# Four heads per slot in tiles without relative scores, and one program for the shared and the routed experts

## The reference

```python
q, k, v = (proj(W, b) for ...)              # 16 heads of 8
idx = clip(r[None, :] - r[:, None], -128, 128) + 128
scores = (q @ k^T + einsum('bhqd,qkd->bhqk', q, rel_k[idx])) / sqrt(8)
w = softmax(scores)
out = w @ v + einsum('bhqk,qkd->bhqd', w, rel_v[idx])
x = x + layernorm(out @ Wo.T + bo)          # its input is layernorm(x)

logits = h @ w_router.T                     # h = layernorm(x), 16 experts, top 1
expert = (up * silu(gate)) @ down_proj[e]   # on sigmoid(score) * h
shared = silu(h @ w_gate.T) * (h @ w_up.T) @ w_down.T
x = x + layernorm(shared + expert)
```

## Time and profile before

| | |
|---|---|
| median of 3 timed runs | 1821.07 us (1820.16 to 1823.48) |
| the profiled execution | 1817.03 us |
| its span, first to last instruction | 1815.3 us |
| mean granted TensorE clock | 0.964 |
| busy: PE, DVE, ACT, POOL | 1625.7, 1256.4, 1107.1, 532.7 us |
| slot loop, first and last exponential | 135.0 to 1463.9 us |
| second block, first load | 1594.0 us |

### The profile page before, as it was taken

One profiled execution on the slowest core, in us unless ns is written; L12 is line 12 of the kernel. 1 busy time (PEld: TensorE's weight loads), 2 busy tenths in 40 slices (PEclk: granted clock), 3 DMA queues, 4 the chain that ended last, 5 costly groups with the idle time before them and its releaser, 6 DMA issues. The chain is left out here.

```text
span 1815.3 us, 64460 instructions
## 1 busy us (share of the span) xinstructions
PE 1625.7 (90%) x26621; PEld 1209.2 (67%) x26621; DVE 1256.4 (69%) x3502; ACT 1107.1 (61%) x2059; POOL 532.7 (29%) x1114
## 2 busy tenths in 40 slices
PE   2889999999999999999999999999999988776672
PEld 1337767676777677767776777777677765476662
DVE  5996668787778878777878787877753444246555
ACT  2437767676767676767676766777557632265441
POOL 5422021314142223222321323231101135604435
PEclk9999999999999999999999999999999998889876
DMA  2467855756553555445444654563357342243420
GB/s 61 143 168 201 178 164 109 198 106 166 103 146 69 131 101 145 96 117 128 98 112 104 143 105 120 99 158 53 66 99 209 73 116 69 63 111 95 128 90 26
DMA packets 490854, 211.89 MB, mean 117 GB/s; under 512 B 332391, under 2 KB 464164, under 8 KB 490560
## 3 DMA queue, kind: packets, MB, share of 16 engines
q1 hardware_dynamic: 475968, 165.77, 40.6%
q0 software_dynamic: 14592, 42.00, 6.7%
HBM read 105.73 MB, written 102.85 MB: 115 GB/s over the span
## 5 line engine op out<-in xcount | busy, mean ns | idle before, releaser
L934 ACT ACTIVATE w<-sc,escale 128x512 f32<-128x512 f32 x1024 | 686.1, 686 | 400.6 <-PE sc L731 248.5
L1135 DVE TENSOR_REDUCE mx<-mix 128x1 f32<-128x512 f32 x960 | 646.8, 686 | 242.5 <-PE mix L711 233.1
L710 PE MATMUL mix<-WE 128*128 128x512 f16 x960 | 395.7, 412 | 23.7 <-DVE mx L1135 15.6
L724 PE MATMUL sc<-QC,KC 104*128 104x128 f16 x4096 | 400.6, 221 | 6.2 <-ACT w L934 3.5
L750 PE MATMUL pv<-w,VC 128*9 128x128 f32 x8192 | 380.7, 274 | 2.1 <-issue 2.1
L724 PEld LDWEIGHTS sc<-QC,KC 104*128 104x128 f16 x4096 | 270.6, 98 | 164.1 <-issue 74.3
L711 PE MATMUL mix<-Wn,WE 128*128 128x256 f16 (+1 forms) x960 | 289.4, 301 | 0.0
L750 PEld LDWEIGHTS pv<-w,VC 128*9 128x9 f32 x8192 | 174.5, 90 | 144.6 <-issue 128.9
L925 ACT ACTIVATE WE<-qp,hmask 128x256 f16<-128x256 f16 x512 | 249.0, 500 | 24.7 <-PE sc L711 21.2
L757 PE MATMUL rel<-w,Rv 128*32 128x128 f32 x5120 | 259.4, 273 | 0.5 <-issue 0.5
L731 PE MATMUL sc<-QT,Wt 96*128 96x64 f16 x5120 | 258.5, 192 | 0.0
(11 more groups left out here) (224 smaller groups left out, 1846.6 us busy)
## 6 DMA issues: line engine op xcount, KB each, us to landing
qm_d<-ks POOLq DMA_DIRECT2D x48, 512.0 KB, 4.4
QT<-qm_d SPq DMA_DIRECT2D x32, 768.0 KB
kt_d<-ks SPq DMA_DIRECT2D x48, 256.0 KB
KC<-kt_d SPq DMA_DIRECT2D x128, 96.0 KB
xs_d<-zrow SPq DMA_DIRECT2D x5, 2056.0 KB, 12.3
vs_d<-vst SPq DMA_DIRECT2D x16, 576.0 KB
VC<-vs_d SPq DMA_DIRECT2D x32, 288.0 KB
orl_d<-rel_s SPq DMA_DIRECT2D x512, 8.0 KB
```

The costliest lines, as they stand in the source:

```text
L710: nc.tensor.matmul(nat[:], lq, kn[b2][:, KEYS_AT[t]:KEYS_AT[t] + S], start=True, stop=False, skip_group_check=True)
L724: mm = nc.tensor.matmul(bank[:, P * g:P * g + P], KC[j][:, b2, g, 0 if near else 1, :], qc[:, g, :, 32 * q8:32 * q8 + 32], start=(g == 0), ...
L934: nc.scalar.activation(w[tile % 2][:, slot % 4, slot // 4 % 2].rearrange("p h q -> p (h q)"), sc[slot % 2][:], ACT.Exp, scale=escale[:, 0: ...
L1135: nc.vector.tensor_reduce(mx[:, k:k + 1], nat[:], AX.X, ALU.max).then_inc(s["mx_done"], 1)
```

## The change

1. In far tiles a slot is now one group of four heads against all 128 queries, and `scores` makes one matmul of 512 columns. `exponentials` writes it to the same layout of `w`, so in pieces of 32 queries: `p h u q` is read, `p u h q` is written. `values` is unchanged.
2. `expert_phase` is gone. Its instructions stand at the end of each engine's program in the first block. Its tiles use the banks of the slot loop, and its buffers lie in one tensor, `shared_part`, over those of keys, queries and values. The ring of weights has 7 places. SyncE's order is new, the matmul and the reads of the expert numbers lie between the last units, and the first weight copies ahead of the last unit's `copy_y`.
3. The two roots of the last half pair run on VectorE, and the steps are no longer in GpSimd's order between the units' scatters.
4. The root of a group takes 12 steps instead of 15, and the last group is finished in two halves of four tiles (`ENDINGS`).

```diff
-            for g in range(4):
-                mm = nc.tensor.matmul(bank[:, P * g:P * g + P], KC[j][:, b2, g, 0 if near else 1, :], qc[:, g, :, 32 * q8:32 * q8 + 32],
-                                      start=(g == 0), stop=not near, skip_group_check=True)
+            if not near:
+                mm = nc.tensor.matmul(bank[:], KC[j][:, b2, q8, 1, :], qc[:, q8], start=True, stop=True, skip_group_check=True)
             if near:
+                for g in range(4):
+                    nc.tensor.matmul(bank[:, P * g:P * g + P], KC[j][:, b2, g, 0, :], qc[:, g, :, 32 * q8:32 * q8 + 32],
+                                     start=(g == 0), stop=False, skip_group_check=True)
...
+            if abs(tile // 4 - tile % 4) <= 1:
+                weights, products = w[tile % 2][:, part, b2].rearrange("p h q -> p (h q)"), sc[slot % 2][:]
+            else:
+                weights = w[tile % 2][:, :, b2, 4 * part:4 * part + 4, :].rearrange("p u h q -> p h u q")
+                products = sc[slot % 2][:].rearrange("p (h u q) -> p h u q", h=4, u=NS)
...
+        sp.wait_ge(s["s_done"], SLOTS * NP)
+        sp.wait_ge(s["pv_done"], SLOTS * NP)
+        sp.wait_ge(scat, 64 * 2 * NP)
+        for g in range(2):
+            load_rows(g)
+        for r in range(4):
+            sp.wait_ge(unit_st[r], 16 * NT * (UNITS // 4))
+        for g in range(2):
+            load_ysh(g)
+        for g in range(2):
+            load_x1(g)
+        for g in range(2, GROUPS):
+            load_rows(g)
+            load_ysh(g)
+            if g > 2:
+                load_x1(g - 1)
+        load_x1(GROUPS - 1)
...
+        pe.wait_ge(s["cnt_read"], 2 * NP)
+        pe.wait_ge(m["cnt_step"], 3)
+        nc.tensor.matmul(mix[1][:, 0:P], ones[:], diag[:], start=True, stop=True).then_inc(m["cnt_ps2"], 1)
+        gates_and_ups(UNITS - 1)
+        downs(UNITS - 2)
         downs(UNITS - 1)
...
+        def expert_downs(n):
+            pe.wait_ge(m["h_done"], n + 1)
+            if n == 2:
+                pe.wait_ge(s["unit_out"], UNITS)
+            at_least(pe, m["y_ev"], n - 3)
...
+        for n in range(AHEAD):
+            expert_weights(n)
         copy_y(UNITS - 1)
+        copy_rows(0)
...
+            if u in (4, 5):
+                base = NEWTON_STEPS * (2 * (2 * last + 1) + u - 4)
+                dve.wait_ge(s["ln_step"], 12 * (2 * last + 1) + 6 * (u - 3))
+                for k in range(NEWTON_STEPS):
+                    dve.wait_ge(s["root2"], base + k)
+                    newton_step(nc.vector, k, rstd2, var2, rtmp2, c15).then_inc(s["root2"], 1)
...
-        for u in range(3):
-            scatter_unit(u)
-        root2(NP - 1, 1, 0)
-        scatter_unit(3)
-        root2(NP - 1, 1, 1)
-        for u in range(4, 11):
+        for u in range(11):
             scatter_unit(u)
         scatter(NP - 1, 1)
         for u in range(11, UNITS):
             scatter_unit(u)
...
-RING = 8
+RING = 7
...
+REFINE_STEPS = 3 + 9
+ENDINGS = [(g, 0, GROUP) for g in range(GROUPS - 1)] + [(GROUPS - 1, 0, GROUP // 2), (GROUPS - 1, GROUP // 2, GROUP // 2)]
```

More of the change, by code:

```diff
@@ L26 @@
 from contextlib import ExitStack
+import math
 import concourse.bass as bass
@@ L933, in exponentials @@
                 at_least(act, "pv_done", SLOTS * i + 8 * (tile - 1))
-            nc.scalar.activation(w[tile % 2][:, slot % 4, slot // 4 % 2].rearrange("p h q -> p (h q)"), sc[slot % 2][:], ACT.Exp,
-                                 scale=escale[:, 0:1]).then_inc(s["exp_done"], 1)
+            part, b2 = slot % 4, slot // 4 % 2
+            if abs(tile // 4 - tile % 4) <= 1:
[3 more added lines that the diff above has]
+                products = sc[slot % 2][:].rearrange("p (h u q) -> p h u q", h=4, u=NS)
+            nc.scalar.activation(weights, products, ACT.Exp, scale=escale[:, 0:1]).then_inc(s["exp_done"], 1)
         def outputs(n, t, b2):
@@ new lines, in places @@
+        def places(g):
+            num = x1g[g % 2][:, :, D]
+            dve.wait_ge(x1_ld[g % 2], 16 * (g // 2 + 1))
+            at_least(dve, out_st[g % 2], 16 * GROUP * (g // 2))
+            nc.vector.scalar_tensor_tensor(out=oidx_f[g % 2][:], in0=num, scalar=0.0, in1=pad[:], op0=ALU.is_equal, op1=ALU.mult).then_inc(m["oidx_step"], 1)
+            dve.wait_ge(m["oidx_step"], 2 * g + 1)
+            nc.vector.scalar_tensor_tensor(out=oidx_f[g % 2][:], in0=num, scalar=1.0, in1=oidx_f[g % 2][:], op0=ALU.subtract, op1=ALU.max).then_inc(m["oidx_step"], 1)
+            dve.wait_ge(m["oidx_step"], 2 * g + 2)
+            nc.vector.tensor_copy(oidx[g % 2][:], oidx_f[g % 2][:]).then_inc(m["oidx_rdy"], 1)
@@ new lines, in expert_normalize @@
+        def expert_normalize(f, quarter):
+            g, k0, size = ENDINGS[f]
+            if quarter == 0:
+                dve.wait_ge(m["root3"], REFINE_STEPS * (f + 1))
+                if k0 == 0:
+                    at_least(dve, out_st[g % 2], 16 * GROUP * (g // 2))
+            for k in range(k0 + size // 4 * quarter, k0 + size // 4 * (quarter + 1)):
+                ins = nc.vector.tensor_scalar(og[g % 2][:, k, :], yg[g % 2][:, k, :], mv3[g % 2][:, k, 0:1], rstd3[g % 2][:, k:k + 1], ALU.subtract, ALU.mult)
+            ins.then_inc(m["fin_step"], 1)
@@ new lines, in residual, with ending @@
+        def residual(f, half):
+            g, k0, size = ENDINGS[f]
+            dve.wait_ge(m["fin_step"], 4 * f + 2 * half + 2)
+            tiles = slice(k0 + size // 2 * half, k0 + size // 2 * (half + 1))
+            nc.vector.tensor_tensor(og[g % 2][:, tiles, :], og[g % 2][:, tiles, :], x1g[g % 2][:, tiles, 0:D], ALU.add).then_inc(m["out_rdy"], 1)
+        def ending(f, step, third):
+            g, k0, size = ENDINGS[f]
+            since = step - (GROUP * g + k0 + size + 5)
+            if 0 <= since < REFINE_STEPS // 3:
+                refine(f, 3 * since + third)
+            since -= REFINE_STEPS // 3
+            if third == 2:
+                if since == -1 and k0 == 0:
+                    places(g)
+                if since == 2:
+                    residual(f, 0)
+                if since == 4:
+                    residual(f, 1)
+                if 0 <= since < 4:
+                    expert_normalize(f, since)
@@ new lines, in _ @@
+        for n in range(SORTED + 5 + REFINE_STEPS // 3 + 5):
+            for third in range(3):
+                for f in range(len(ENDINGS)):
+                    ending(f, n, third)
+                if third == 0 and n < SORTED:
+                    expert_hidden(n)
+                if third == 1 and 0 <= n - 3 < SORTED:
+                    add_shared(n - 3)
+            if 0 <= n - 5 < SORTED:
+                mean_and_variance(n - 5)
+            if 0 <= n - 4 < SORTED:
+                expert_moments(n - 4)
@@ L1549, in _, with store_rows @@
             scatter_unit(u)
+        def store_rows(f):
+            g, k0, size = ENDINGS[f]
+            if k0 == 0:
+                pool.wait_ge(m["oidx_rdy"], g + 1)
+            for k in range(size):
+                if k % (size // 2) == 0:
+                    pool.wait_ge(m["out_rdy"], 2 * f + 2 * k // size + 1)
+                pool.indirect_dma_start(out.rearrange("b s d -> (b s) d"), bass.IndirectOffsetOnAxis(ap=oidx[g % 2][:, k0 + k:k0 + k + 1], axis=0),
+                                        og[g % 2][:, k0 + k, :], None, bounds_check=TOK - 1, oob_is_err=False).then_inc(out_st[g % 2], 16)
+        for f in range(len(ENDINGS)):
+            store_rows(f)
         pool.wait_ge(scat, 64 * 2 * NP)
@@ L1552, in _ @@
             pool.wait_ge(unit_st[r], 16 * NT * (UNITS // 4))
+        for r in range(2):
+            pool.wait_ge(out_st[r], 16 * GROUP * (GROUPS // 2))
 IDENT_READY = 3
```

427 lines of the change are left out of this document (158 added, 269 removed).

## The result

The changed kernel takes 1800.05 us (median of 8 runs, 1797.75 to 1809.48), the one before 1819.73 (8 runs). The medians differ by 19.7 us.

| from ...

A forecast was written before the change was run, and what follows sets the result against it. TensorE's columns bound the slot loop, waits the last 350 us. Sum 1817.0 - 1.5 - 4 - 11 - 10 = 1790.5, with 4.0 to the median 1794.5, say 1795; range 1766 to 1814, own case 1783 to 1803.

The forecast's parts named there:

- the roots: Shared experts: moving the last half pair's root steps from GpSimd into VectorE's gaps saves 4 us, bounds 0 and 7.
- the boundary: Between shared experts and sorted tiles: without a second block, early tiles start before ysh is there; 11 us saved, bounds 6 and 12.
- the loads: Sorted tiles: two loads instead of three meet each scatter stream; 1.5 us per group, -10, bounds 0 and -17; whole cause -50.
- Bound of the slots, and the join: Slot loop: TensorE's columns bound it, so joining four score matmuls in far slots saves 1.5 us, at most 3.8.
- Rival C: Far slots: the exponential's write in 32-element pieces costs 0.31 us each, half exposed gives 1855 us; chance 0.05.
- rival E: Far slots: one joined matmul streams faster than its columns, giving about 1747 us; chance 0.02.
- the reservation that GpSimd also waits for unit outputs: Shared experts: because of these waits, not all of the 7 us taken off GpSimd comes back.
- within 5 us of ysh's issue: Sign for the boundary term: sorted tile 6 starts within 5 us of the issue of the ysh load.
- rival A: Only the boundary goes: late reports depend on scatters alone, GpSimd's gain is eaten by TensorE's waits; 1808.5 us, chance 0.26.
- Endings: End of groups: three fewer root steps per group and the last group in two halves gain nothing.

The follow-up runs named there:

- e1: The kernel before with only the far tiles' joined 512-column score matmul and exponential written in pieces of 32, first chip: 1815.02 us, ratio 0.9974.
- e2: The changed kernel with the two roots of the last half pair back on GpSimd between unit scatters 3 and 4, first chip: 1804.91 us, ratio 0.9914.
- e3: The changed kernel with SyncE's loads from group 2 on in the old order (rows, x1, shared rows), first chip: 1799.06 us, ratio 0.9880.
- e11: The kernel before, unchanged, on a fourth chip, where reports are on time: 1733.63 us.
- e10: The changed kernel itself, run again on a third chip, where reports are on time: 1718.85 us, ratio 0.9901.
- e5: The changed kernel with the old endings (15 root steps, last group in one piece), second chip: 1718.08 us, ratio 0.9901.

## Why the prediction was right, and where it was not

The time lay in the stated range, and two of the three terms that made most of the forecast, the roots and the boundary, were there by their stated mechanism. The third, the loads, was not. The time still fell within 1783 to 1803, with 3 us to spare, because the other two came nearly whole; the width of the range took in what the mechanism had wrong.

*Bound of the slots, and the join.* Right: turns two to seven of the four traces with the change in its slots (after, e1, e2, e3) give 1.9 to 4.6 us for 384 joined matmuls, forecast 1.5 of at most 3.8. In the recorded pair the last turn was 1.8 us longer after, so that only 0.3 us reached the last exponential. Rival C (write in pieces) is out by 688 ns, rival E by 0.23 us from a joined matmul to the next. The Trainium skill (TensorE: Matmul & The Clock Gate, Back-to-back issue gap) has 131 ns per matmul of 512 columns in a stream of load and matmul pairs; the measured 0.23 us decides against it here.

*Roots, -4.* Right in size where reports are late: -5.2, and +6.6 when put back. Between e11 and e10 it was +3.1. There the reservation that GpSimd also waits for unit outputs came true, and the argument that VectorE takes the steps in its gaps did not hold, by the timelines of e10 and e11.

*Boundary, -11.* Right mechanism and nearly the size: -8.1 in the trace after, -9.7 in e2 (12.3 us instead of 22.0), -11.1 in e3 (10.8), -10.4 on time. As forecast, TensorE had started only three tiles' gates when ysh was issued, held back by the scatters. Tile 6 did not start within 5 us of ysh's issue at 1588.09 but 8.6 after, as the load took 5.7 to the first add and tiles 3 to 5 came first.

*Loads in the steady part, -10.* This step failed, and by it the forecast time was too low. It took from the earlier trace rows that three loads beside the scatters make the late reports worse, and put 1.5 us a group on the third. e3 gives that load back to the scatters and loses nothing; the 0.5 us a group of the trace after are inside the 6 us by which e1 and before differ in an unchanged stage. The reading of the earlier trace rows, that scatters alone are enough, was the right one, and rival A's (chance 0.26) in this point. That nothing in the loads matters was not shown: the kernels without loads ran where no report was late, and where reports are on time the order of the loads is worth some 4 us by another route, the late ysh of e11. The term's bounds were not sound either: a third of 9.3 us in 7 groups is 22 us and not 17, and all of it 65 and not 50.

*Endings, 0.* Off by +1.7 in the trace after, and likewise in e2 (33.1) and e3 (33.9) against 31.7 and 31.5 (e1); on time -1.3 by e5. Argued, not shown: 12 root steps bring each stream of scatters forward, so the eighth, at 1761.75, meets the gates of both tiles 78 and 79 (from 1762.45 and 1763.79), where before it began at 1780.44, with those of tile 78 already on since 1779.66. e5 ran where there are no late reports and could not decide it.

*Sum.* By the terms as measured, -2.5 - 5 - 9.5 + 0 + 1.7 = -15.3, beside 17.5 (14.4 to 20.4) timed. The forecast of 26 was too large, in the main by the one term of 10. That this sum lies near the 15.5 of the table is partly luck: the table has 0.3 for the join and 3.6 in the sorted tiles, and the latter is less than two traces of that stage differ by.

## What to carry to other kernels

When two things coincide with a stall, and one of them is seen with the stall alone elsewhere in the same trace, give the other no share of the price until it has been moved. In a stage that follows the pace of one engine's reports, indirect scatters are better spread over the tiles than issued eight in a row: 35 us here on one chip, nothing lost on another. Work taken off an engine that is waiting for inputs anyway comes back as a wait; ask what it will reach earlier, and whether that is there. Ask too what the work stands ahead of on the engine that gets it: a low busy share (VectorE, 45.02 of 123 us) does not say that the steps fall into a gap.

## What the hardware showed that was not expected

The same kernel takes 1820 us on one chip and 1733.6 to 1736.3 on three others, with the slot loop's costliest instructions equal within 1% (an exponential 686 and 687 ns). Of the 83.8 us between the spans of before (1815.3) and e11 (1731.5), 60.1 lie in sorted tiles 8 to 79, 16.3 between the last exponential and the last shared scatter, 5.6 up to the last exponential. On the first chip and in the recorded runs instructions wait for TensorE's results 3 to 5 us past their modelled ends while GpSimd issues scatters 1.3 us apart (in after the silu at 1649.70, with gates that end at 1646.92, and the one at 1586.26, with gates that end at 1580.88); on the others, with the same stream of scatters, they do not wait. After TensorE has waited, its granted clock falls too (0.84 and 0.89 on the mean of that stage in before and after, at 2.4 GHz and by turns at 1.2; 1.00 in e10), and the mean of a gate matmul is 305 ns in after and 278 in e10. Why one chip differs is open.
